# A new timetable for four chained attention blocks: the 8-head value product leaves the score bank for four rotating banks

## The reference, cut to what matters

```python
weight = softmax(einsum('bhct,bhcs->bhts', q * scale, k * scale))
a = einsum('bhts,bhcs->bhct', weight, v)
return x + proj(a)
```

## Time and profile before

| what | value |
|---|---|
| median of 3 runs | 2110.87 us (2109.59 to 2112.22) |
| the profiled execution | 2112.12 us |
| its span, first to last instruction | 2109.7 us |
| busy: TensorE / ScalarE / VectorE / GpSimd | 2011.4 / 1886.4 / 1843.0 / 973.3 us |
| mean granted clock of TensorE | 0.98 |

### The profile page before, as it was taken

How to read it: one execution, slowest core, us unless ns; L and a number is a source line. 1 busy time by engine, 2 the same in 40 slices (tenths; PEclk the granted TensorE clock), 3 DMA queues, 4 the chain that set the end, 5 groups by cost and what they waited for, 6 DMA issues and landing times.

```text
span 2109.7 us, 57712 instructions
## 1 busy us (share of the span) xinstructions
PE 2011.4 (95%) x15232; PEld 1689.6 (80%) x15232; DVE 1843.0 (87%) x4683; ACT 1886.4 (89%) x6231; POOL 973.3 (46%) x1707
## 2 busy tenths in 40 slices
PE   4589999999999999999999999999999999999977
PEld 3367888888888888888888888888888888888766
DVE  6789999999999999999999999999999999997532
ACT  2269999999999999999999999999999999999984
POOL 3544544545444454544445454444545544453211
PEclk8799999999999999999999999999999999999988
DMA  4000011001101100110111011011101101000000
GB/s 129 16 24 24 17 40 40 24 30 38 38 23 38 38 30 24 38 38 23 38 38 36 18 38 38 23 38 38 38 15 38 38 27 34 31 32 17 24 24 39
DMA packets 29819, 70.31 MB, mean 33 GB/s; under 512 B 6252, under 2 KB 7088, under 8 KB 29744
## 3 DMA queue, kind: packets, MB, share of 16 engines
q1 hardware_dynamic: 26928, 67.68, 9.1%
q10 hardware_dynamic: 2816, 1.72, 0.3%
HBM read 30.85 MB, written 12.85 MB: 21 GB/s over the span
## 4 chain that ended last, share of the span: by engine, by line
PE 88%; ACT 4%; DVE 1%; issue 1%; DVEq 0%; ACTq 0%
PE ps_e L1167 21%; PE ps_c L1167 21%; PE ps_b L1167 15%; PE ps_a L1167 11%; PE ps_s L1167 10%; PE ps_s L1222 8%; ACT e L830 1%; PE ps_a L1469 1%; ACT e L822 1%; ACT pt L836 0%; PE ps_e L1298 0%; PE ps_a L1298 0%; DVE nm L958 0%; ACT e L877 0%; ACT kv L742 0%
## 5 line engine op out<-in xcount | busy, mean ns | idle before, releaser
L822 ACT ACTIVATE e<-ps_s,nm 98x196 f32<-98x196 f32 x1024 | 423.9, 436 | 36.2 <-DVE nm L958 32.0
L830 ACT ACTIVATE e<-e,rden 98x196 f32<-98x196 f32 x1024 | 403.2, 462 | 0.2 <-DVE rden L1063 0.2
L1159 DVE SCALAR_TENSOR_TENSOR y<-opad,w_dw,y 128x406 f32<-128x406 f32 x512 | 314.9, 666 | 0.0
L1140 DVE SCALAR_TENSOR_TENSOR y<-xpad,w_dw,y 128x406 f32<-128x406 f32 x512 | 298.4, 636 | 0.0
L587 POOL TENSOR_SCALAR xn<-x,gn_scale,gn_shift 128x196 f32<-128x196 f32 x384 | 286.1, 757 | 20.8 <-POOL gn_shift L582 20.8
L575 POOL TENSOR_TENSOR gn_t<-gn_group 128x4 f32<-128x4 f32 x96 | 27.7, 289 | 563.7 <-DVE gn_group L1008 430.1
L958 DVE TENSOR_REDUCE nm<-ps_s 98x4 f32<-98x784 f32 x256 | 239.4, 966 | 34.2 <-PE ps_s L1167 34.2
L836 ACT COPY pt<-ps_s 98x392 f32<-98x392 f32 x512 | 233.3, 502 | 4.7 <-PE ps_s L1222 2.8
L1222 PE MATMUL ps_s<-w_eye,e 98*98 98x98 f32 x2048 | 228.9, 249 | 7.3 <-ACT e L830 7.2
L1222 PEld LDWEIGHTS ps_s<-w_eye,e 98*98 98x98 f32 x2048 | 200.5, 130 | 38.8 <-issue 22.3
L822 ACT ACTIVATION_READ_ACCUMULATOR e<-ps_s,nm 98x1 f32 x1024 | 222.7, 217 | 0.0
(11 more groups left out here) (223 smaller groups left out, 5326.6 us busy)
## 6 DMA issues: line engine op xcount, KB each, us to landing
x_in<-in_x SPq DMA_DIRECT2D x32, 392.0 KB, 3.2
x_res<-in_x SPq DMA_DIRECT2D x32, 392.0 KB, 3.1
x2b<-x SPq DMA_DIRECT2D x32, 392.0 KB, 2.7
out<-x SPq DMA_DIRECT2D x32, 392.0 KB, 2.6
out_pairs<-out SPq DMA_DIRECT2D x32, 392.0 KB, 2.5
w_q<-in_q SPq DMA_DIRECT2D x3, 256.0 KB
w_k<-in_k SPq DMA_DIRECT2D x3, 256.0 KB
w_v<-in_v SPq DMA_DIRECT2D x3, 256.0 KB
```

What stands on the lines that cost most here:

```text
L822: s.activation(e2[:, j, tc], tile(use)[0:HALF, of_image(tc)], ACT.Exp, bias=nm2[:, j, tc:tc + 1], accum_out=den2[:, 2 * i + tc, h:h + 1]). ...
L830: s.activation(e2[:, j, tc], e2[:, j, tc], ACT.Copy, scale=rden2[:, 2 * i + tc, h:h + 1]).then_inc(p2_done[j].sem, 1)
L1140: v.scalar_tensor_tensor(out=dst, in0=window(xpad, c, k, CR), scalar=tap, in1=dst, op0=ALU.mult, op1=ALU.add).then_inc(conv1_steps.sem, 1)
L1159: v.scalar_tensor_tensor(out=dst, in0=window(opad, c, k, CR), scalar=tap, in1=dst, op0=ALU.mult, op1=ALU.add).then_inc(conv2_steps.sem, 1)
```

## The change

Three things change. `av{g}` gets a home in the plain banks: av0 in a, av1 and av2 in c, av3 in e. The names in the plain banks are dealt out anew. And all numbers of PE_AT, ACT_AT, DVE_AT and of GpSimd's `probs` are new, so TensorE, ScalarE and VectorE run other cyclic orders; SP_AT and the instructions themselves, their shapes and their number stay as they are. With the new numbers `av2, av3, av0` stand directly behind `sc3, sc0, sc1` on TensorE, while `sc2` and `av1` stand alone.

The banks:

```diff
 BANK_USES = {
-    "a": ("t0_1", "o0_1", "gn1", "ctx0", "hv0", "gn3", "v3_2", "v3_0", "t3_0", "t3_1", "o3_1",),
-    "b": ("k0", "v0", "o0_0", "mlp0", "q1_0", "ctx1", "out1", "v3_1", "v3_3", "s3_1",),
-    "c": ("q0_0", "s0_0", "pw0", "kv1", "kv3", "q1_1", "hq0", "hq1", "hk1", "q3_0", "s3_0", "o3_0",),
-    "e": ("q0_1", "s0_1", "t0_0", "pw1", "mlp1", "kv0", "kv2", "out0", "gn2", "hk0", "hv1", "proj1",
-          "proj0", "q3_1",),
+    "a": ("s0_0", "t0_0", "o0_0", "gn1", "q1_0", "ctx0", "out1", "hk1", "av0", "proj1", "v3_0", "q3_0", "o3_0",),
+    "b": ("q0_1", "k0", "t0_1", "mlp0", "kv0", "out0", "hk0", "hv0", "q3_1", "v3_3", "s3_1", "t3_0", "t3_1",),
+    "c": ("v0", "mlp1", "kv1", "kv2", "q1_1", "ctx1", "gn2", "hq1", "av1", "av2", "v3_1", "s3_0", "o3_1",),
+    "e": ("q0_0", "s0_1", "o0_1", "pw0", "pw1", "kv3", "hq0", "hv1", "av3", "proj0", "gn3", "v3_2",),
 }
...
             use for g in range(GROUPS) for use in (
-                (f"sc{g}_{j}", PE_AT[f"sc{g}"], 2), (f"tn{g}_{j}", PE_AT[f"tn{g}_{j}"], 1),
-                *([(f"av{g}", PE_AT[f"av{g}"], 1)] if j == 0 else []))]) for j in range(HG)]
+                (f"sc{g}_{j}", PE_AT[f"sc{g}"], 2), (f"tn{g}_{j}", PE_AT[f"tn{g}_{j}"], 1))]) for j in range(HG)]
```

The tables' lines from which the orders below follow (TensorE's new one whole, of the others the part from sc0 to ctx1):

```diff
 PE_AT = {
+    "q0_1": 106, "q0_0": 113, "k0": 121, "s0_0": 145, "s0_1": 147, "t0_0": 166, "v0": 172, "t0_1": 184, "o0_0": 189,
+    "o0_1": 195, "pw0": 248, "pw1": 268, "mlp0": 283, "mlp1": 285, "gn1": 309, "kv0": 341, "kv1": 342, "kv3": 344,
+    "kv2": 345, "q1_0": 350, "q1_1": 361, "ctx0": 367, "ctx1": 368, "out1": 372, "out0": 374, "gn2": 397, "hk0": 421,
+    "hq0": 426, "sc0": 438, "hv0": 447, "hk1": 453, "hv1": 454, "tn0_1": 455, "tn0_0": 458, "tn0_2": 460, "hq1": 462,
+    "tn0_3": 464, "sc1": 467, "av0": 468, "tn1_0": 484, "tn1_3": 486, "tn1_2": 487, "tn1_1": 488, "sc2": 492,
+    "av1": 499, "tn2_0": 508, "tn2_3": 519, "tn2_1": 521, "tn2_2": 522, "sc3": 526, "av2": 527, "tn3_1": 546,
+    "tn3_0": 547, "tn3_3": 551, "tn3_2": 553, "av3": 567, "proj1": 591, "proj0": 594, "gn3": 619, "q3_1": 658,
+    "v3_0": 660, "v3_2": 670, "q3_0": 673, "v3_1": 676, "v3_3": 691, "s3_0": 697, "s3_1": 717, "t3_0": 727,
+    "t3_1": 754, "o3_1": 759, "o3_0": 779,
...
 ACT_AT = {
+    "bn0": -43, "bn1": 3, "q0_1": 121, "q0_0": 127, "k0": 149, "exp0_0": 162, "exp0_1": 170, "t0_0": 180, "v0": 186,
...
 DVE_AT = {
+    "conv1_0": 7, "conv1_1": 44, "conv1_2": 48, "conv1_3": 49, "conv1_4": 54, "conv1_5": 62, "conv1_6": 64,
+    "conv1_7": 70, "conv1_8": 71, "s0_0": 146, "s0_1": 159, "sum0_0": 162, "sum0_1": 170, "conv2_0": 202,
...
 POOL_AT = {
-    "resize0": 96, "resize1": 112, "probs0": 160, "probs1": 176, "gn1": 336, "gn2": 400, "gn3": 640, "rows3": 704,
+    "resize0": 96, "resize1": 112, "probs0": 175, "probs1": 181, "gn1": 336, "gn2": 400, "gn3": 640, "rows3": 704,
```

## The result

The changed kernel takes 2173.32 us (median of 4 runs, 2168.59 to 2175.42), the kernel before 2111.05 on the same chip: ratio 1.0292, 95% interval 1.0276 to 1.0307. The profiled execution spans 2166.8 us at a mean granted clock of 0.979. The forecast was 2118 us, at most 2146: slower was right, the size was not.

The account below looks back on a forecast made before the run. TensorE bounds the old kernel at 61.29 us a pair; afterwards the VectorE-ScalarE chain, 31.26, plus 30.28 back gives 61.54. 29 pairs by 0.25 add 7 us: 2118 for the median, range 2085 to 2146.

Parts of the forecast that it names:

- TensorE first: TensorE's tiled groups: merging eight into five saves 0.54 to 0.99 us a pair; TensorE alone needs 60.1 to 60.6.
- The chain: sc0 to ctx1 through VectorE and ScalarE: 1.04 + 15.83 + 0.99 + 13.40 = 31.26 us, against TensorE's own 29.9 to 30.2.
- the way back: TensorE from ctx1 to the next sc0: 30.2 to 30.35 us, taken as 30.28, against 32.05 before.
- the 1.1 us that ctx1 was to stand: TensorE at ctx1: about 1 us of waiting in each pair, for ScalarE's keys.
- VectorE's stretch: VectorE from max0_0 to max1_0: 15.83 us, or 15.5 with a quick conv2_1.
- Rival 2: GpSimd's gn1 starts late beside taps and becomes the wait: 0.4 to 1.5 us more a pair, 2130 to 2162; chance 0.16.
- the first half: The part of a pair from sc0 to ctx1, forecast at 31.26 us.
- What was put at nothing: Waits for readers from plain products' new bank homes, above all VectorE's av, priced at zero; some tenths a pair if cover goes.
- Theory C: Posed for the experiments, without a chance: merged segments and new bank homes cost TensorE itself.

Follow-up runs that it names:

- Run 10: The changed kernel with one merge undone: av2 goes behind s0_0, so sc3 and av2 are separate tiled segments; 2173.46 us, ratio 1.0292.
- run 5: The changed kernel with VectorE's taps conv1_2 to conv1_8 cut to one row, order and signals kept; 2086.49 us, ratio 0.9874 to the kernel before.
- run 1: The changed kernel with layer 1's split reading x1, not xn1, so ScalarE's high1 does not wait for gn1; 2117.66 us, ratio 1.0032.
- run 6: The changed kernel with av3, s3_0's reduction and rden0_0 behind max0_1 on VectorE, ahead of taps conv1_2 to conv1_4; 2145.64 us, ratio 1.0166.
- run 4: The changed kernel with gn1's matmul ahead of v0, its copy ahead of max0_0, v3_3 in bank e ahead of hk0; 2146.74 us, ratio 1.0164.
- run 8: run 1's kernel with VectorE's conv2_1 moved out of the stretch before max1_0: behind av0 2127.62 us, behind kv1 2130.81 us.
- run 9: Four full versions of the changed kernel with conv2_1 moved behind av0 or kv1 and other reorderings, three with gn1 early; 2142.32, 2134.14, 2139.09, 2301.93 us.
- run 7: run 6's kernel with tap conv1_2 also moved ahead of gn1's copy on VectorE; 2119.83 us, ratio 1.0045 to the kernel before.
- run 2: The changed kernel with taps conv1_2 and conv1_3 back ahead of max0_0 on VectorE; 2148.13 us, ratio 1.0175 to the kernel before.

## Why the prediction failed, step by step

**TensorE first: held, at the low end.** sc3 and av2 behind one another take 0.85 + 0.80 us (937.84 to 939.49), as much as they took apart. So the step from sc to av is not free, and only av's entry and the next product's penalty go: 0.18 by the prediction's sum, not the 0.25 that I took. The Trainium skill (TensorEngine Tiling (Array Packing), Key Properties) says that a change of tiling mode drains the engine; the trace agrees in that the merged groups are no shorter. Run 10 adds that of this one merge some 0.07 was left in the pair. In run 5, where the profile lists no wait of TensorE, ctx0 to ctx1 still takes 1.99 (996.88 to 998.87) instead of 1.75; without these 0.24 TensorE needs at most 60.6, the upper end of the forecast's 60.1 to 60.6.

**The chain: held.** With gn1 out of the way (run 1) sc0 to ctx1 takes 31.31 against 31.26 forecast, the way back 30.29 against 30.28, and the kernel 2117.66 against 2118. The gain on TensorE would not have arrived in any case. The place of the wait was wrong: of the 1.1 us that ctx1 was to stand, 0.65 stand at t3_0, and 0.24 at ctx1 (955.41 to 957.40 from ctx0, against 1.75 before), which starts 0.05 after keys3 ends. And that VectorE's stretch comes so near, 15.78 against 15.83, is in part luck: from start to start conv2_1 took 1.18 instead of its old 1.41, conv2_0 0.88 instead of 0.70.

**Rival 2, gn1 on GpSimd: this is the step that failed.** In the sum VectorE's stretch from max0_0 to max1_0 stands at 15.83, with no wait for gn1 in it; it took 17.33. I named the wait as a rival, gave it 0.16 and 0.4 to 1.5 us, and it cost the first half 1.63; it should have been in the sum. Its three numbers: the start was to be 0.2 to 1.7 after sc0 and was 1.99; the block was taken at its old 10.69 and was 11.26; VectorE's low1_1 alone was to be 0 to 0.4 late. In fact low1_0 and low1_1 waited 0.87 and 0.17, and conv2_0, now beside the resize, took 1.34 against 0.96 in run 1; with the overlap of starts lost at both waits (0.16) that is 1.58, and the stretch grew by 1.50 over the forecast, 1.55 over run 1. (By the other road, over sc1, max1_0 could not have come earlier either.) I also asked only when VectorE wants low1. high1 stands earlier in ScalarE's queue, 1.81 us ahead of xn, and hv1, less0_3 and tn0's copies stand behind it; through them TensorE's sc1 came 17.33 after sc0 instead of 14.94.

**Why the block is that long: the taps.** Of the two reasons named in the rival, late start and taps beside it, runs 5 and 6 separate them: same start, block 5.2 and 7.70, no wait. In run 4 the block is 9.66 long and starts earlier, and nothing waits for it either: as far as these runs go, the wait takes the late start and the long block together. In the old order it was almost the same block, and it did not matter, since it began 1.2 us ahead of sc0 and not 1.99 behind it, and low1_0 stood behind conv2_1. The price of the taps could be read there already. The prediction sets the four xn steps beside two taps without a break; those were conv1_6 and conv1_7, with rden0_0 and av3 between them. The two taps without a break, conv1_4 and conv1_5 (1051.40 to 1053.69), ran beside a small step of the kernel before:

```profile
1050.71 3.04 POOL L581 TENSOR_TENSOR gn_t<-gn_group,gn_scale 128x4 f32<-128x4 f32 x1
```

In the changed kernel it is another step that is caught, and the block is as long as it was.

**What was put at nothing.** The new homes: the forecast named readers of av, mlp1 and o3_1, and these cost nothing visible. The ones that count are kv0 ahead of t3_0 and kv2 ahead of q1_1, which bind once gn1 does not (runs 1, 8, 9). As the source of the 1.63 us Theory C falls with runs 1 and 5.

**Still open:** whether some order gets the 60.85 of run 5 with the full work. Run 7 gets to 61.5. VectorE is busy 925 of 1000 us in run 1, and apart from conv1_2 ahead of gn1's copy, where VectorE stood anyway (run 7), every place to which I moved a tap was one where something waits for VectorE.

## What to carry to other kernels

When a table of work is dealt anew, sum the chain around the meeting points, with every engine in it: a slow engine's block is a link as soon as its start or its deadline moves, and its length has to be taken with its new neighbours. Ask of a late result not only who reads it, but what stands behind that reader on its engine. And an instruction moved out of one chain lands in another: before moving it, look which buffer's reader it will stand in front of.

## What the hardware did that I had not expected

A GpSimd step on four numbers per partition took 2.90 us where two full taps, four VectorE instructions, followed max0, and ended 0.06 us after the last of them. With the taps cut to one row (run 5) the same step, at the same point of max0, took 0.20; it took 0.20 too where no tap came directly behind max0 (runs 2 and 6). The kernel before has the same with another step, 3.04 us, and again 0.06 after the fourth instruction. But not every step beside taps is held so long: gn_scale, gn_t and gn_shift, beside the eight instructions of conv1_5 to conv1_8 (960.67 to 965.28), took 0.63, 0.47 and 0.48. What decides between the two is not shown.

The four scalings took 3.78 us beside full taps, 2.05 in run 5 with its cut ones. The taps pay as well: three of them beside the scalings took 3.62 in run 6, where 2.29 for two makes some 3.4 (an estimate).

The Trainium skill (SBUF — State Buffer, Who interferes with whom) has a lock between a VectorE instruction with two SBUF inputs and a GpSimd instruction that reads SBUF, held for the whole instruction. The trace agrees that taps and GpSimd steps hold each other up and that max0, which reads PSUM, does not; that one step stays held through four instructions, and others do not, goes beyond it.
